# A decoder layer: loads issued by ScalarE instead of SyncE, two copies moved to VectorE, and new orders of work

## The chip, the cores and the metric

The kernel runs on one core of a Trainium2 chip. The metric is the device time of one execution in microseconds. The engines are called as in the profile: PE (TensorE), DVE (VectorE), ACT (ScalarE), POOL (GpSimd), SP (SyncE, which here only issues DMAs); "SPq" is the time of SP's queue in issuing them.

## The reference

One decoder layer in float32, for 32 batches of 112 rows of 256 numbers, with a context of 375 rows of 256 per batch:

```python
x = x + attn(layernorm(x), wq, wk, wv, wo)       # 8 heads of 128, q and k rms-normalised and rotated, causal
x = x + xattn(layernorm(x), ctx, ctx)            # gelu(xn @ ctx.T) @ ctx, per batch
x = x + ffn(layernorm(x), w1, b1, w2, b2)        # 256 -> 1024 -> 256, values rounded to 8 bits, relu
```

## The kernel before

Every engine has its own program: small functions, each one step for one batch `j` (a wait or several on semaphores, one or a few instructions, an increment of a semaphore), and three lists that call them, `start()`, `body(i)` for i from 5 to 25, and `end()`. The lists are written out by hand, and an engine goes through its list strictly in order. So a step that waits holds all that stand behind it on its engine. PSUM's eight banks are shared between steps, and part of the waits guard a bank until the step that read it is done.

The attention's input is laid out in tiles of 128 rows: eight batches of 112 rows make seven tiles, so 28 of the 32 batches have a tile of their own (`has_tile`), and in the other four the steps that work on tiles fall away. Precision is kept by splitting float32 values into two float16 parts (high, and the rest), which triples the matmuls of the projections, the scores and the output projection.

The steps of a batch, in the order in which its data passes, with the engine:

- SP `load_rows` brings the tile (`x_rows`); DVE `stats_x`, POOL `variance_x` and `root_x`, DVE `normalise_x` make `xn1`; ACT `round_xn` (L1455) makes its high half and DVE `split_xn` (L817) its low half; SP `transpose_x` is a DMA that transposes both into `xT16`.
- PE `project_q`, `project_k`, `project_v0`, `project_v1` (L1745). q and k go through ACT `square`, DVE `turn_cos`, `turn_sin`, `sum_squares`, the rotation's sum (DVE `turn_q`, POOL `turn_k`), POOL `rms_root`, ACT `scale` and `round`, DVE `split`, and then through DMA transposes issued by SP: `transpose_q`, `transpose_k`, and `transpose_q_next`, `transpose_k_next` for the rows of the tile that belong to the next batch.
- PE `scores`, ACT `softmax_exp`, POOL `mask_later_keys`, PE `weigh_values`, DVE `invert_sums`, ACT `normalise_o0`, `normalise_o1`, `round_o`, DVE `split_o` (L947), SP `transpose_o` (L321, a DMA), PE `project_out0` to `project_out3` (L1755), DVE `residual_attention`, which adds `x_in`, brought by SP `load_x` (L330).
- DVE `stats_x2`, POOL `root_x2`, DVE `normalise_x2`, PE `transpose_xn2`, ACT `copy_xn2T` (L1407, from PSUM to SBUF), PE `ctx_hidden` on the transposed context (`ctxT`, SP `load_ctxT`, L309), ACT `square_h`, DVE `gelu_inner`, ACT `tanh_h`, DVE `gelu_outer`, PE `ctx_out` on the context's rows (SP `load_ctx`, L335), DVE `residual_ctx`.
- DVE `stats_x3`, POOL `root_x3`, DVE `quantise_x3`, `clip_x3`, SP `transpose_xq` (a DMA), PE `hidden_units0`, `hidden_units1`, ACT `relu0`, `relu1`, DVE `clip_hidden`, PE `out_units`, POOL `add_b2`, DVE `residual_out`, SP `store_out`.

The steps of one round of `body` belong to several batches: on PE the projection of q runs three batches ahead of the round's number, `weigh_values` one ahead, `project_out` one behind, `out_units` four behind. All DMAs, of the weights too, are issued by SP, on one queue; those of one round are, in order: `load_ctxT`, `load_rows`, `transpose_o`, `transpose_x`, `load_x`, `load_ctx`, `transpose_q`, `transpose_k`, `transpose_q_next`, `transpose_xq`, `store_out`, `transpose_k_next`. Three of the loads wait until their buffer is free:

```python
def load_ctxT(j):
    if j.has(2):
        sp.wait_ge(h_ready, done(j.plus(-2)))
def load_x(j):
    if j.has(2):
        sp.wait_ge(x2_done, done(j.plus(-2)))
def load_ctx(j):
    if j.has(2):
        sp.wait_ge(ctxout_ready, done(j.plus(-2)))
```

Before the first batch, the weights are squared and summed (ACT `square_projection`, `square_wo`; PE `sum_weights`), scaled by a power of two, and rounded and split into halves (ACT `round_projection`, DVE `split_projection`).

Of the kernel before, what the change touches and what calls it, by code (L numbers as in the profile page):

```python
# [18 lines left out]
P = 128  # L19
BANK = 512  # L20
SLOTS = 4
# [42 lines left out]
def done(j):  # L64

    return j.off + 1
# [35 lines left out]
def decoder_layer(nc, x, ctx_rows, ctx_cols, wq, wk, wv, wo, w1_cols, b1, w2_cols, b2, tables, out):  # L102
# [30 lines left out]
    with ExitStack() as stack:  # L133
# [92 lines left out]
        y_ps = psum[0:T, 6, 0:M]  # L226
        xn2T_ps = psum[:, 2, 0:MC * T]
        h_ps = psum[0:SP, 2, 0:SC * T]
        ctx_ps = psum[0:T, 7, 0:M]
        f0_ps, f1_ps = psum[:, 0, 0:FC // 2 * T], psum[:, 1, 0:FC // 2 * T]  # L230
        f2_ps = psum[0:T, 7, 0:M]
# [40 lines left out]
        def _(sp):  # L272
# [33 lines left out]
            def load_ctxT(j):  # L306
                if j.has(2):
                    sp.wait_ge(h_ready, done(j.plus(-2)))
                sp.dma_start(ctxT[:, j.off % 2], ctx_cols[j.at].rearrange("o (c p) s -> (o p) c s", p=P)).then_inc(  # L309
                    ctxT_landed[j.off % SLOTS], 16)  # L310

            def load_rows(j):
                if 3 <= j.off <= 4:
                    sp.wait_ge(xn_done, done_t(j.plus(-2)))
                sp.dma_start(x_rows[:, tile_no(j) % 2, :], x_flat[tile_no(j)]).then_inc(rows_landed[tile_no(j) % 2], 16)

            def transpose_o(j):
                if j.has(1):
                    sp.wait_ge(y1_added, done(j.plus(-1)))
                sp.wait_ge(o_lo_done, done(j))  # L320
                sp.dma_start_transpose(oT16[:, :, :], o16[:, :, :].rearrange("t l n -> t (l n)")).then_inc(oT_landed, 16)  # L321

            def transpose_x(j):
                sp.wait_ge(xn_lo_done, done_t(j))
                sp.dma_start_transpose(xT16[:, :, tile_cols(j)], xn16[:, :, :].rearrange("t l n -> t (l n)")).then_inc(xT_landed, 16)

            def load_x(j):
                if j.has(2):
                    sp.wait_ge(x2_done, done(j.plus(-2)))
                sp.dma_start(x_in[:, j.off % SLOTS, :], x[j.at].rearrange("o t m -> (o t) m")).then_inc(x_landed[j.off % SLOTS], 16)  # L330

            def load_ctx(j):
                if j.has(2):
                    sp.wait_ge(ctxout_ready, done(j.plus(-2)))
                sp.dma_start(ctx_in[:, j.off % 2], ctx_rows[j.at].rearrange("o (p c) m -> (o p) c m", c=SC)).then_inc(  # L335
                    ctx_landed[j.off % SLOTS], 16)

            def transpose_q(j):
                sp.wait_ge(q_lo_done, done_t(j))
                own, cut = own_rows(j)  # L340
                sp.dma_start_transpose(qkT[:, j.off % 2, 0, :, PAD + own:PAD + T], qk16[0:cut, 0].rearrange("t l n -> t (l n)")).then_inc(qT_landed, 16)  # L341

# [5 lines left out]
            def transpose_q_next(j):  # L348
                sp.wait_ge(q_lo_done, done_t(j))
                if j.has(1):  # L350
                    sp.wait_ge(s_ready, done(j.plus(-1)))
                own, cut = own_rows(j)
                for a, b in pieces_after(cut):
                    sp.dma_start_transpose(qkT[:, (j.off + 1) % 2, 0, :, PAD + a - cut:PAD + b - cut],  # L354
                                           qk16[a:b, 0].rearrange("t l n -> t (l n)")).then_inc(qT_next_landed, 16)
# [1816 lines left out]
```

## Time and profile before

| what | value |
|---|---|
| median of 3 runs | 658.45 us (656.49 to 659.91) |
| the profiled execution's own time | 658.12 us |
| its span, from the first to the last instruction | 656.1 us |
| mean granted clock of TensorE | 0.972 |
| busy: PE, DVE, ACT, POOL | 583.0, 533.7, 526.5, 382.2 us |

Busy is the time in which an engine has an instruction in execution; the issuing of DMAs doesn't count. A batch with a tile takes about 18 us in the middle of the run, and the span is longer than 32 times the mean round by the filling and the draining of the pipeline.

### The profile page before, as it was taken

Reading aid. Unit: us, or ns where it says so; the run is one execution under the profiler, and the core shown is the slowest. Engines: PE = TensorE matmul, PEld = TensorE weight load, DVE = VectorE, ACT = ScalarE, POOL = GpSimd, SP = SyncE. Lnnn points to the kernel's source line nnn. Section 1 sums busy time; section 2 is a strip of 40 time slices with the busy share of each in tenths; the row PEclk is TensorE's granted clock in tenths of the full one; section 3 lists DMA queues with packets and bytes.
Section 4 is the critical chain, followed back from the end, with each engine's and each line's share of the span. In section 5 each row is a group of like instructions: output and inputs, shape, how many; then the busy total and the mean of one; then the engine's idle time right before and its main releaser. Section 6 shows DMA issues by size and latency. Waiting matters only on the chain.

```text
span 656.1 us, 13024 instructions
## 1 busy us (share of the span) xinstructions
PE 583.0 (89%) x4528; PEld 440.0 (67%) x4528; DVE 533.7 (81%) x1059; ACT 526.5 (80%) x1350; POOL 382.2 (58%) x402
## 2 busy tenths in 40 slices
PE   1678699898999999989999999989998888799984
PEld 1324367676777777776787777757777556589873
DVE  3898689797899998986999999967997879584653
ACT  6888689695899998994999999976898778696643
POOL 1445466582677776763678877733776649352321
PEclk9887799999999999999999999989999989899998
DMA  8665764898799999989889899998798969979551
GB/s 297 203 135 120 102 111 87 143 124 167 144 141 169 159 155 154 148 158 174 125 166 152 146 157 156 158 147 178 102 162 130 168 97 130 107 165 167 152 123 29
DMA packets 236720, 95.25 MB, mean 145 GB/s; under 512 B 210144, under 2 KB 231248, under 8 KB 236656
## 3 DMA queue, kind: packets, MB, share of 16 engines
q1 hardware_dynamic: 236656, 94.43, 82.3%
q8 instruction: 36, 0.59, 0.4%
q14 instruction: 28, 0.23, 0.1%
HBM read 39.08 MB, written 3.67 MB: 65 GB/s over the span
## 4 chain that ended last, share of the span: by engine, by line
PE 41%; SPq 22%; DVE 13%; DMA 8%; POOL 6%; ACT 6%; issue 3%; ACTq 0%; DVEq 0%
PE psum L1750 6%; PE psum L1751 5%; PE psum L1752 5%; PE psum L1911 4%; SPq L354 4%; PE psum L1880 3%; PE psum L1796 3%; SPq L321 3%; DMA qkT<-qk 3%; SPq L373 3%; SPq L346 3%; SPq L341 2%; PE psum L1758 2%; PE psum L1760 2%; PE psum L1759 2%
## 5 line engine op out<-in xcount | busy, mean ns | idle before, releaser
L1750 PE MATMUL psum<-wqkv,xT 128*128 128x512 f16 (+1 forms) x352 | 139.3, 396 | 16.7 <-DVE wqkv L772 9.3
L1751 PE MATMUL psum<-wqkv,xT 128*128 128x512 f16 (+1 forms) x352 | 138.8, 394 | 0.0
L1752 PE MATMUL psum<-wqkv,xT 128*128 128x512 f16 (+1 forms) x352 | 138.5, 393 | 0.0
L578 POOL TENSOR_TENSOR turn_c<-turn_c,turn_s 128x1024 f32<-128x1024 f32 x28 | 80.1, 2859 | 25.2 <-DVE turn_c L746 19.4
L753 DVE TENSOR_TENSOR turn_s<-psum,sin_t 128x1024 f32<-128x1024 f32 x56 | 68.0, 1216 | 11.9 <-ACT sq L1330 11.7
L1758 PE MATMUL psum<-wo,oT 128*112 128x256 f16 x256 | 70.0, 273 | 5.2 <-DMA oT<-o 5.2
L1750 PEld LDWEIGHTS psum<-wqkv,xT 128*128 128x128 f16 (+1 forms) x352 | 39.8, 113 | 51.0 <-DVE wqkv L772 9.5
L1760 PE MATMUL psum<-wo,oT 128*112 128x256 f16 x256 | 69.8, 273 | 0.0
L1759 PE MATMUL psum<-wo,oT 128*112 128x256 f16 x256 | 69.8, 273 | 0.0
L603 POOL TENSOR_TENSOR rms<-ms,nhalf 128x8 f32<-128x8 f32 x28 | 68.2, 2436 | 2.2
L595 POOL TENSOR_TENSOR rstd<-ve,nhalf 112x1 f32<-112x1 f32 x32 | 26.4, 826 | 72.7 <-DVE ve L864 72.7
L746 DVE TENSOR_TENSOR turn_c<-psum,cos_t 128x1024 f32<-128x1024 f32 x56 | 68.1, 1216 | 0.5 <-ACT sq L1427 0.4
L1752 PEld LDWEIGHTS psum<-wqkv,xT 128*128 128x128 f16 (+1 forms) x352 | 39.8, 113 | 40.9 <-issue 5.9
L1911 PE MATMUL psum<-v_sb,wo_raw 112*112 112x129 f32 x512 | 63.3, 275 | 2.6 <-issue 2.0
L1302 ACT ACTIVATE qk<-w_raw 128x1024 f16<-128x1024 f32 x56 | 59.6, 1064 | 3.5 <-DMA qkT<-qk 3.1
L1911 PEld LDWEIGHTS psum<-v_sb,wo_raw 112*112 112x112 f32 x512 | 58.8, 176 | 4.9 <-issue 3.5
L1751 PEld LDWEIGHTS psum<-wqkv,xT 128*128 128x128 f16 (+1 forms) x352 | 39.9, 113 | 32.9 <-issue 4.7
L1849 PE MATMUL psum<-qkT 128*112 128x112 f16 x256 | 42.9, 219 | 15.0 <-DMA qkT<-qk 13.6
L1434 ACT ACTIVATE w_raw<-turn_c,rms 128x128 f32<-128x128 f32 x112 | 35.8, 392 | 21.3 <-POOL rms L603 17.8
L1880 PE MATMUL psum<-ctx_all,g 125*112 125x256 f32 x192 | 48.7, 390 | 2.2 <-DVE g L955 1.6
L573 POOL TENSOR_TENSOR rms<-ms,nhalf 128x8 f32<-128x8 f32 x28 | 48.4, 1727 | 2.2
L1368 ACT ACTIVATE f_int<-psum,b_col 128x112 int16<-128x112 f32 x128 | 34.7, 360 | 16.9 <-PE psum L1868 16.9
(108 smaller groups left out, 1634.6 us busy)
## 6 DMA issues: line engine op xcount, KB each, us to landing
ctxT<-in_ctx_cols SPq DMA_DIRECT2D x32, 375.0 KB, 4.1
ctx_all<-in_ctx_rows SPq DMA_DIRECT2D x32, 375.0 KB
x_rows<-in_x SPq DMA_DIRECT2D x28, 128.0 KB, 3.8
x_in<-in_x SPq DMA_DIRECT2D x32, 112.0 KB, 2.7
out_y<-y_out SPq DMA_DIRECT2D x32, 112.0 KB, 2.1
w_raw<-in_w SPq DMA_DIRECT2D x2, 1024.0 KB, 6.2
qkT<-qk SPq DMA_TRANSPOSE x128, 4.3
w_raw<-in_wk SPq DMA_DIRECT2D x2, 512.0 KB, 4.8
```

The lines of the kernel that those rows point to most:

```text
L578: pool.tensor_tensor(turn_c[:, 1, :], turn_c[:, 1, :], turn_s[:, 1, :], ALU.add).then_inc(k_turned, 1)
L603: pool.tensor_tensor(rms[:, 0, :], ms[:, 0, :], nhalf[:, 0:H], ALU.pow).then_inc(q_rms_done, 1)
L746: return dve.tensor_tensor(turn_c[:, w, :].rearrange("t (h f) -> t h f", f=HALF), ps.rearrange("t b (h f) -> t (b h) f", f=HALF), table, A ...
L753: return dve.tensor_tensor(turn_s[:, w, :].rearrange("t (h two f) -> t h two f", two=2, f=HALF), halves, table, ALU.mult)
L1750: pe.matmul(dst, hi, wqkv[:, 0, c, w, cols], start=c == 0, stop=False)
L1751: pe.matmul(dst, hi, wqkv[:, 1, c, w, cols], start=False, stop=False)
L1752: last = pe.matmul(dst, lo, wqkv[:, 0, c, w, cols], start=False, stop=c == MC - 1)
L1758: pe.matmul(y_ps, oT16[:, h, :], wo16[:, 0, h, :], start=first and h == heads[0], stop=False)
L1759: pe.matmul(y_ps, oT16[:, h, :], wo16[:, 1, h, :], start=False, stop=False)
L1760: product = pe.matmul(y_ps, oT16[:, H + h, :], wo16[:, 0, h, :], start=False, stop=last and h == heads[-1])
L1880: last = pe.matmul(ctx_ps, g[:, c * T:(c + 1) * T], ctx_in[:, j.off % 2, c, :], start=c == 0, stop=c == SC - 1)
L1911: last = pe.matmul(o_ps[:, h // OH, at:at + VW], p_sb[:, h * T:(h + 1) * T], v_sb[:, h, :], start=h % OH == 0, stop=h % OH == OH - 1 or h ...
```

## The change

- `load_rows`, `load_ctxT`, `load_x` and `load_ctx` are issued by ACT, on its own DMA queue. The waits of `load_ctxT` and `load_x` are gone (the order of ACT's other steps stands in for them). SP keeps the weights, the transposes and the stores.
- `round_xn` and `copy_xn2T` run on DVE as `tensor_copy`.
- All lists are laid out anew, and PSUM's banks with them: `scores` and `v0`, `out_units` share banks, `weigh_values` and q, `ctx_hidden` and `ctx_out`, and `w_sum_ps` now lies in a bank of `k_ps`. So the first `project_k` waits for the last of the weights' sums, `w_sq_done[3]`, that of wo. The waits that guard banks follow.
- In the loop, on PE, q runs one batch ahead of the round's number, `weigh_values` one behind, `project_out` two behind, `transpose_xn2` three, `ctx_out` four, `out_units` five. `project_out` begins with `project_out2`.

```diff
-        q_ps, k_ps = psum[:, 4:6, :], psum[:, 0:2, :]
-        v0_ps, v1_ps = psum[0:T, 7, :], psum[0:T, 3, :]
-        s_ps = psum[0:T, 0:2, 0:HH * T]
-        o_ps = psum[0:T, 4:7, 0:OH * VW]
+        q_ps, k_ps = psum[:, 1:3, :], psum[:, 5:7, :]
+        v0_ps, v1_ps = psum[0:T, 4, :], psum[0:T, 3, :]
+        s_ps = psum[0:T, 4:6, 0:HH * T]
+        o_ps = psum[0:T, 0:3, 0:OH * VW]
...
+            def load_rows(j):
+                if j.has(2):
+                    act.wait_ge(xn_done, done_t(j.plus(-2)))
+                act.dma_start(x_rows[:, tile_no(j) % 2, :], x_flat[tile_no(j)]).then_inc(rows_landed[tile_no(j) % 2], 16)
...
+            def load_ctxT(j):
+                act.dma_start(ctxT[:, j.off % 2], ctx_cols[j.at].rearrange("o (c p) s -> (o p) c s", p=P)).then_inc(
+                    ctxT_landed[j.off % SLOTS], 16)
...
+            def load_x(j):
+                act.dma_start(x_in[:, j.off % SLOTS, :], x[j.at].rearrange("o t m -> (o t) m")).then_inc(x_landed[j.off % SLOTS], 16)
...
+            def load_ctx(j):
+                if j.has(2):
+                    act.wait_ge(ctxout_ready, done(j.plus(-2)))
+                act.dma_start(ctx_in[:, j.off % 2], ctx_rows[j.at].rearrange("o (p c) m -> (o p) c m", c=SC)).then_inc(
+                    ctx_landed[j.off % SLOTS], 16)
...
+            def round_xn(j):
+                dve.wait_ge(xn_done, done_t(j))
+                if j.has(1):
+                    dve.wait_ge(xT_landed, 16 * done_t(j.plus(-1)))
+                dve.tensor_copy(xn16[:, 0, :], xn1[:, :]).then_inc(xn_hi_done, 1)
...
+            def copy_xn2T(j):
+                dve.wait_ge(xn2T_ready, done(j))
+                dve.tensor_copy(xn2T[:, :, :].rearrange("p c t -> p (c t)"), xn2T_ps).then_inc(xn2T_copied, 1)
```

The loops after the change, in order, without the conditions on tiles (c is the batch i+1, d i, e i-1, f i-2, g i-3, h i-4, and i itself i-5; a and b are i+3 and i+2):

```
SP    transpose_q d, transpose_q_next d, transpose_k d, transpose_o e, transpose_k_next d, transpose_x a,
      store_out i, transpose_xq g
PE    project_q c, ctx_out h, transpose_xn2 g, hidden_units1 i, hidden_units0 i, scores e, ctx_hidden g,
      project_out2 f, project_out0 f, project_out1 f, project_out3 f, out_units i, weigh_values e,
      project_k c, project_v0 d, project_v1 d
ACT   square_h h, scale_k1 e, scale_k0 e, tanh_h h, round_k0 e, normalise_o0 f, normalise_o1 f, round_o f,
      square_k d, copy_v0 e, load_rows a, scale_q0 d, load_ctxT f, copy_v1 e, scale_q1 d, load_x e, square_q c,
      relu1 i, relu0 i, load_ctx f, round_q0 d, softmax_exp e
DVE   normalise_x b, turn_q d, split_k e, gelu_outer h, split_o f, turn_cos_k d, normalise_x2 g, turn_sin_k d,
      round_xn b, sum_squares_k d, residual_ctx h, copy_xn2T g, stats_x3 h, stats_x a, turn_sin_q c,
      clip_hidden1 i, quantise_x3 h, clip_x3 h, clip_hidden0 i, split_xn b, turn_cos_q c, sum_squares_q c,
      gelu_inner g, residual_attention f, residual_out i, split_q d, invert_sums e, stats_x2 f
POOL  root_x3 i, rms_root_k e, mask_later_keys f, variance_x b, root_x b, add_b2 i, rms_root_q d, root_x2 g,
      turn_k d
```

In `start()`, SP issues wv, wk, wq, wk, wq in halves, then wo, the biases and the other half of wv, and ACT at the same time the first context, two tiles of rows and the first x.

## Rows read from the trace of the kernel before

**Rows 1.** The page: part 1, PE's line, and part 4, the chain by engine.

```profile
PE 583.0 (89%) x4528; PEld 440.0 (67%) x4528; DVE 533.7 (81%) x1059; ACT 526.5 (80%) x1350; POOL 382.2 (58%) x402
...
PE 41%; SPq 22%; DVE 13%; DMA 8%; POOL 6%; ACT 6%; issue 3%; ACTq 0%; DVEq 0%
```

**Rows 2.** Windows of one batch, 18 of them, 181.30 to 505.63: busy us, clock, DMA.

```profile
342.31:360.25 17.94, 17.94 (x148) 13.81 (x145) 17.16 (x35) 16.73 (x46) 14.04 (x13) 1.00 0.95 158
...
sum 324.33, PE 316.51 PEld 243.99 DVE 290.43 ACT 284.21 POOL 224.33; mean PE 17.58 PEld 13.55 DVE 16.13 ACT 15.79 POOL 12.46
```

**Rows 3.** Windows of 30 us: length, then busy us by engine as in rows 2.

```profile
0.00:30.00 30.00, 10.73 (x40) 6.09 (x40) 16.10 (x36) 21.35 (x29) 7.73 (x21) 0.99 0.80 268
...
540.00:570.00 30.00, 23.97 (x191) 17.79 (x192) 21.39 (x35) 22.62 (x56) 18.82 (x16) 0.94 0.85 122
```

**Rows 4.** Waits of PE: who waited for whom, us in total, times, longest.

```profile
PE psum L1849 <- DMA qkT<-qk: 13.6, 9, 4.3
...
PE psum L1868 <- DMA xqT<-xq: 6.1, 2, 3.3
...
PE psum L1758 <- DMA oT<-o: 5.2, 3, 2.4
```

**Rows 5.** Timeline of SP in the undisturbed batch: start, us of issuing, line.

```profile
343.41 0.57 SPq L330 DMA_DIRECT2D x_in<-in_x  x1
344.03 0.33 SPq L335 DMA_DIRECT2D ctx_all<-in_ctx_rows  x1
...
347.55 3.39 SPq L346 DMA_TRANSPOSE qkT<-qk  x1
...
355.48 1.34 SPq L309 DMA_DIRECT2D ctxT<-in_ctx_cols  x1
356.87 0.47 SPq L315 DMA_DIRECT2D x_rows<-in_x  x1
357.43 2.73 SPq L321 DMA_TRANSPOSE oT<-o  x1
```

**Rows 6.** Groups by line and shape: busy us, mean ns, idle before.

```profile
L817 DVE TENSOR_TENSOR xn<-xn 128x256 f16<-128x256 f32 x28 | 16.1, 575 | 1.6 <-ACT xn L1302 1.6
...
L920 DVE SCALAR_TENSOR_TENSOR y_out<-psum,x3b 112x256 f32<-112x256 f32 x32 | 13.2, 412 | 8.6 <-PE psum L1788 8.6
...
L1302 ACT ACTIVATE xn2T<-psum 128x224 f32<-128x224 f32 x32 | 12.0, 374 | 4.1 <-PE psum L1765 3.9
...
L1302 ACT ACTIVATE xn<-xn 128x256 f16<-128x256 f32 x28 | 11.4, 408 | 0.5 <-DVE xn L932 0.3
...
L804 DVE TENSOR_SCALAR b_rows<-b_clip 112x256 f32<-112x256 f32 x1 | 0.3, 286 | 0.0
```

**Rows 7.** Timeline of PE in a batch: start, us, line (weigh_values, out_units, project_out).

```profile
181.31 1.98 PE L1911 MATMUL psum<-v_sb,wo_raw 112*112 112x129 f32 x16
...
185.91 1.04 PE L1788 MATMUL psum<-w2T,f_q 128*112 128x256 bf16 x8
...
188.08 0.27 PE L1758 MATMUL psum<-wo,oT 128*112 128x256 f16 x1
188.19 0.27 PE L1759 MATMUL psum<-wo,oT 128*112 128x256 f16 x1
```

**Rows 8.** Timelines of ACT and DVE in the undisturbed batch: normalise_o1, round_o, split_o.

```profile
345.99 1.16 ACT L1421 ACTIVATE wo_raw<-psum,rden 112x128 f32<-112x128 f32 x4
...
351.19 1.04 ACT L1302 ACTIVATE o<-wo_raw 112x1024 f16<-112x1024 f32 x1
...
352.58 1.22 DVE L947 TENSOR_TENSOR o<-wo_raw,o 112x1024 f16<-112x1024 f32 x1
```

**Rows 9.** The tile oT: its transposes, from issue to landing.

```profile
DMA to landing us min/median/max: 4.0/5.4/8.5
```

**Rows 10.** DMA issues: the load of wo, us from issue to landing last.

```profile
wo_raw<-in_wo SPq DMA_DIRECT2D x1, 1024.0 KB, 10.3
```

**Rows 11.** Timeline of PE at the start: the first project_k.

```profile
16.96 0.61 PE L1750 MATMUL psum<-wqkv,xT 128*128 128x512 f16 x1 [3.69 <-DVE wqkv L772]
```

More of the change, by code:

```diff
@@ L1423, in normalise_o1, with round_o @@
                 last.then_inc(o1_normed, 1)
+            def round_o(j):
+                act.wait_ge(o1_normed, done(j))
+                if j.has(1):
+                    act.wait_ge(oT_landed, landed_once(j.plus(-1)))
+                act.wait_ge(o0_normed, done(j))
+                copy(o16[:, 0, :], on[:, :]).then_inc(o_hi_done, 1)
             def square_k(j):
@@ L1830, in project_out3, with ctx_out, transpose_xn2 @@
-            def project_out3(j):
-                project_out(range(6, 8), j, first=False, last=False).then_inc(y_ready, 1)
+            def ctx_out(j):
+                pe.wait_ge(ctx_landed[j.off % SLOTS], landed(j))
+                pe.wait_ge(g_done, done(j))
+                for c in range(SC):
+                    last = pe.matmul(ctx_ps, g[:, c * T:(c + 1) * T], ctx_in[:, j.off % 2, c, :], start=c == 0, stop=c == SC - 1)
+                last.then_inc(ctxout_ready, 1)
+            def transpose_xn2(j):
+                pe.wait_ge(xn2_done, done(j))
+                if 1 <= j.off <= B - 10 or j.off == B - 4:
+                    pe.wait_ge(v1_copied, done(j.plus(2)))
+                if j.off == B - 7 or j.off == B - 5:
+                    pe.wait_ge(x2_done, done(j.plus(1)))
+                if j.off == 0:
+                    pe.wait_ge(ident_in, 16)
+                transpose_rows(xn2T_ps, xn2).then_inc(xn2T_ready, 1)
@@ new lines, in hidden_units1 @@
+            def hidden_units1(j):
+                pe.wait_ge(xqT_landed, landed_once(j))
+                if B - 6 <= j.off <= B - 5:
+                    pe.wait_ge(o1_normed, done(j.plus(3)))
+                if j.off == B - 4:
+                    pe.wait_ge(o0_normed, done(j.plus(3)))
+                for c in range(1 * FC // 2, 2 * FC // 2):
+                    for m in range(MC):
+                        last = pe.matmul(f1_ps[:, (c % (FC // 2)) * T:(c % (FC // 2) + 1) * T], w1T[:, m, c, :], xqT[:, m, :],
+                                         start=m == 0, stop=m == MC - 1)
+                last.then_inc(f1_ready, 1)
@@ L1852, in scores, with ctx_hidden @@
                 last.then_inc(s_ready, 1)
-            def project_out2(j):
-                project_out(range(4, 6), j, first=False, last=False).then_inc(y2_added, 1)
-            def project_out1(j):
-                project_out(range(2, 4), j, first=False, last=True).then_inc(y1_added, 1)
-            def hidden_units1(j):
-                pe.wait_ge(xqT_landed, landed_once(j))
-                if j.off <= B - 10:
+            def ctx_hidden(j):
+                pe.wait_ge(ctxT_landed[j.off % SLOTS], landed(j))
+                pe.wait_ge(xn2T_copied, done(j))
+                if j.off == B - 6 or j.off == B - 4:
+                    pe.wait_ge(x3_done, done(j.plus(-1)))
+                for c in range(SC):
+                    for m in range(MC):
+                        last = pe.matmul(h_ps[:, c * T:(c + 1) * T], ctxT[:, j.off % 2, m, c * SP:(c + 1) * SP], xn2T[:, m, :],
+                                         start=m == 0, stop=m == MC - 1)
+                last.then_inc(h_ready, 1)
```

1841 lines of the change are left out of this document (894 added, 947 removed).

## The prediction

> **What bounds the kernel now.** I read the page's first and fourth part first [rows 1]: TensorE is busy for 583 us of a span of 656.1, and no other engine comes near enough to be the bound on average. The chain that ended last spends 41% on PE, but 22% on SPq (SyncE issuing DMAs) and 8% on landings of DMAs. So the kernel has two faces, and windows separate them. Over the 18 batches between 181.30 and 505.63 us TensorE is busy 316.51 of 324.33 us: 7.8 us idle in half of the run [rows 2]. One undisturbed batch there takes 17.94 us, all of it TensorE at full clock, with VectorE at 17.16, ScalarE at 16.73, GpSimd at 14.04 and the DMA engines at a share of 0.95 [rows 2]. This stretch is bound by TensorE, which the change leaves as it is: the matmuls are the same. The rest of the idle 73.1 us (656.1 less 583.0) lies at the two ends: 19.3 us in the first 30 alone and 6.0 in the 30 from 540 [rows 3].
>
> The waits say what TensorE stands for: of its idle time 13.6 us end with the landing of a transposed q or k, 6.1 with that of xq and 5.2 with that of o, 24.9 us together [rows 4]. These transposes are issued by SP, one after the other, between the loads. SP's queue in the undisturbed batch shows loads of 0.57 (x_in), 0.33 (ctx rows), 1.34 (ctxT) and 0.47 us (x_rows), 2.71 together, beside transposes of which one takes 3.39 and another 2.73 us [rows 5]. A load in front of a transpose delays it by its issue, and by its wait where the buffer isn't free yet.
>
> **The change, part by part.** The profiled execution took 658.12 us, 2.0 more than its span, and 0.3 less than the median of the runs (658.45). The sum starts from 658.1. A difference of 0.5% (3.3 us) is about what a measurement of this kernel tells from none.
>
> *Four loads per batch leave SP.* SP gets 2.71 us per batch back, and no transpose stands behind a load's wait on x2_done, h_ready or ctxout_ready. In the undisturbed batches this is worth nothing, since TensorE is never waiting there. What it can reach is the 24.9 us of waits for transposes. Ends: nothing, if the landing is late because the DMA engines are full (a share of 0.95), and 20 us, if the issue decides (a fifth of the 24.9 kept back, since behind an earlier landing the next wait is seldom far). I take 14, nearer the upper end, since the chain counts 22% for issuing and 8% for landing. The Trainium skill, "DMA: Bandwidth & Descriptors", section "Issuing engines are not separate DMA queues", says that DMAs of all issuing engines run on the same 16 DMA engines and interleave, so that a second issuer saves issue time only. By that rule alone the gain would be the lower end; the share of 0.95 agrees with it, the 22% speaks for a real part of issue time.
>
> *ScalarE issues them.* Before, no ScalarE DMA is in the trace. Its work falls by the rounding of xn (0.408) and the copy of xn2T (0.374 us) [rows 6], 0.78 together, to 15.95 in a batch of 17.94: 2.0 us are free. Four issues at SP's prices are 2.71, at the shortest that SP shows (0.33) 1.3. If an issue runs ahead of the arithmetic queued on ScalarE, it costs nothing. So ScalarE comes to 15.95 + 2.71 = 18.7 us in the dear case, without a gap: 0 to +0.7 us for each of 28 batches with a tile, 0 to +20 us. I take 0: x and ctxT are now loaded with no wait in front of them, x_rows and ctx rows wait for things a batch old, and their places are behind copies and ReLUs of some 0.5 to 1 us that keep the engine fed. The cover is the 2.0 us; beyond 0.5 us per issue it is gone.
>
> *VectorE takes the rounding and the copy.* Neither is in the trace. Round_xn lies between 0.286 (a 112x256 f32 copy with a factor, L804) and 0.575 (the 128x256 subtraction to f16, L817); the copy from PSUM between 0.286 and 0.412 (the 112x256 residual from PSUM, L920) [rows 6]. That is 0.57 to 0.99. I take 0.7: the plain copy is nearer to L804, that from PSUM to L920. VectorE comes to 17.16 + 0.7 = 17.9 of 17.94: still under TensorE, but full. Ends: 17.7, which costs nothing, and 18.15, +0.2 us for 28 batches, 6 us.
>
> *The orders.* In the loop a batch now goes from weigh_values to project_out in one round, where it took two. Between the end of weigh_values and the first project_out lies one round less the matmuls of project_out (24 at 0.11 from start to start, 2.6 us), out_units (1.0) and weigh_values (2.0) [rows 7]: 17.94 - 5.6 = 12.3 us. In them o must be normalised (two groups of 1.16), rounded (1.04), split (1.22) [rows 8] and transposed, 5.4 us from issue to landing in the median and 8.5 at most [rows 9]: 10.0 us, 13.1 with the longest. It fits by 2.3 us as long as ScalarE, VectorE and SP come to it at once; behind project_out all else waits, so what it is late is late for the round. Similarly copy_xn2T stands on VectorE between residual_ctx, which waits for ctx_out, and ctx_hidden, which waits for the copy. I charge 2 us for such slips (0 to +10), as most batches keep both margins.
>
> *The start.* The first project_k now shares a PSUM bank with the sums of the weights and waits for w_sq_done[3], so for the load of wo (10.3 us from issue to landing) [rows 10] and its squares, where it started at 16.96 us and waited for w_k alone [rows 11]. With wo issued sixth it can't start before about 20. But TensorE stood idle again in the same 30 us, 19.3 in all, so part is taken from that idle time: 0 to +5, I take +2.
>
> Sum: 658.1 - 14 + 0 + 0 + 2 + 2 = 648.1.
>
> **The rivals.** *The transfers are the limit, not SP.* For it: a DMA share of 0.95 in a batch in which nothing waits, and a k transpose whose issue took 3.39 us. Against it: loads of 0.33 and 0.47 us pass through the same queue in the same batch, so it isn't full throughout, and the chain gives SPq nearly three times the landings' share. The 14 us shrink to some 3, and 2 + 2 take them back: 659, from 656 to 661.
>
> *ScalarE becomes the bound*, on the other side. Its issues last as long as SP's or longer, drawn out as SP's 3.39 us is. The place is between copy_v0 and softmax_exp, the price each microsecond past 2.0 per batch; late exp delays the mask, out_units and weigh_values at once. At 0.9 us per issue (between SP's 0.33 and 1.34) it is 3.6, less 2.0 a plus of 1.6 for 28 batches, 45 us, with the 10 us gained elsewhere 693; it decides from 2.4 us of issues per batch, where the 10 us are eaten. For it: ScalarE's 16.73. Against it: 0.33 to 0.57 for three of four of SP's loads. The Trainium skill, "Perfetto Trace Analysis", section "DMA Instruction — HWDGE (DVE, Sync)", has a sequencer wait for a lock on a descriptor generator that two of them share, and the profile's duration includes that wait; no row here shows two issuers, so it can't be seen whether ScalarE would stand behind a 3.39 us transpose.
>
> *The loop of o or VectorE sets the round.* If o's transpose lands a microsecond later than the median at each batch, or VectorE waits 0.5 us more than its fullness allows, the round is 0.5 us longer: 28 x 0.5 = 14, so 648 + 14 = 662, and up to 672 where both meet. For it: landings up to 8.5. Against it: SP has 2.71 us less to do.
>
> *The ends shorten too.* SP's relief gives all 20 us and the fill and drain, shorter by the round that o saves, some 10 more: 658 - 20 - 10 = 628, up to 636. Against it: the first matmul is later, and the drain is one chain through all engines.
>
> **How the numbers follow.** SP relieved, covers hold: 0.44, 648, from 638 to 655. Transfers the limit: 0.14, within 0.5%. ScalarE the bound: 0.21, 665 to 720. The loop of o or VectorE: 0.13, counted as slower. The ends too: 0.08. Faster 0.44 + 0.08 = 0.52, same 0.14, slower 0.21 + 0.13 = 0.34. The range from 632 to 680 leaves out half of the last case (0.04) and what of ScalarE's lies above 680 (0.13); the likeliest case's own is 638 to 655.
>
> **What would show it.** Right: SPq's share of the chain falls well under 22%; PE's waits for qkT, xqT and oT fall from 24.9 to near 11 us; a batch in the middle still takes 17.9 to 18.0 with PE busy throughout, VectorE near 17.9; ScalarE's DMA issues last under 0.5 us and nothing on it waits behind them; the first project_k starts past 20 us. Wrong: rounds of 18.3 us or more; ScalarE's queue in the chain with issues near or over 1 us; PE idle before project_out for oT in each round; or the same waits for qkT at the same length with SP idle before them, which would make it the transfers.

## The result and the profile after

The changed kernel takes 726.77 us (median of 4 runs, 725.50 to 729.12) where the kernel before took 657.47 beside it: a ratio of 1.105, 95% interval 1.101 to 1.110. The forecast was 648, from 632 to 680, with "faster" at 0.52. It was wrong in sign and by 79 us. (The profiled executions of a_early_exp, a_early_late_exp and a_early_wsum, below, were disturbed by the chip, so of these three only the ratio, which leaves such executions out, is used for the time.)

The page of the changed kernel, part 1 and the chain by engine of part 4, as in [rows 1]:

```profile
PE 604.2 (83%) x4528; PEld 462.7 (64%) x4528; DVE 544.9 (75%) x1119; ACT 514.7 (71%) x1290; POOL 355.2 (49%) x402
...
PE 31%; DMA 29%; DVE 18%; SPq 12%; ACT 4%; POOL 3%; issue 3%; ACTq 0%; DVEq 0%; POOLq 0%
```

SP's issuing fell from 22% of the chain to 12%, as the change intends. What grew in its place is the landing of DMAs, 8% to 29%. By its share of the span no engine is fuller than before: ScalarE fell to 514.7 us (71%) and VectorE is at 75%.

The waits of PE in the changed kernel, as in [rows 4] (L1839 is scores, L1757 project_out, L1805 hidden_units1):

```profile
PE psum L1839 <- DMA qkT<-qk: 35.0, 12, 10.7
PE psum L1757 <- DMA oT<-o: 20.9, 16, 4.2
...
PE psum L1805 <- DMA xqT<-xq: 4.7, 1, 4.7
```

The three tiles that the prediction wanted to see fall from 24.9 to 11 us rose to 60.6.

Windows from one weigh_values to the next in the changed kernel, 20 of them, from batch 5 (159.06) to batch 25 (557.00), columns as in [rows 2]:

```profile
177.72:195.63 17.91, 17.91 (x146) 13.83 (x145) 14.87 (x33) 14.74 (x40) 10.66 (x13) 1.00 0.45 98
...
455.40:480.51 25.11, 19.86 (x134) 16.34 (x133) 14.47 (x33) 16.02 (x42) 11.68 (x13) 0.80 0.96 114
...
sum 397.94, PE 363.50 PEld 281.75 DVE 322.07 ACT 301.22 POOL 218.69; mean PE 18.18 PEld 14.09 DVE 16.10 ACT 15.06 POOL 10.93
```

And the same 20 batches of the kernel before, in one window:

```profile
145.56:505.63 360.07, 350.54 (x2824) 270.31 (x2821) 318.38 (x644) 310.62 (x820) 240.87 (x241) 1.00 0.93 153
```

Five of the 20 rounds still take 17.9 us, with PE busy throughout. The others take from 16.3 to 25.1 (the shortest is the last, whose steps are mostly those of the list `end()`). Of the 37.9 us that these batches lost, 24.9 are idle time of PE (34.4 now, 9.5 before). The other 13.0 are busy time (363.50 against 350.54) for nearly the same matmuls (2789 against 2824): the granted clock fell from 1.00 to 0.96, and in the round of 25.11 us to 0.80.

Split at the same two batches, the 67.6 us by which the span grew (656.1 to 723.7) are 13.5 before batch 5 (159.06 against 145.56), 37.9 in the 20 rounds, and 16.2 behind batch 25 (166.7 against 150.5). In what follows these are the start, the loop and the drain.

**Where the loop's time goes.** The chain that ended last, in the round of 25.11 us of the changed kernel (start, us, what):

```profile
455.60 0.42 DVE y_out L872
456.02 1.14 DVE qk L877
457.16 0.02 issue
457.18 1.20 SPq L309
...
458.48 1.22 SPq L317
...
459.75 1.32 SPq L317
...
461.11 2.00 SPq L323
...
463.21 12.26 DMA oT<-o
475.47 0.04 issue
475.51 0.46 PE psum L1757
...
479.80 0.87 PE psum L1880 x8
```

It is a circle. L1880 is out_units. When it ends, VectorE can do residual_out (y_out, L872), and behind that split_q (L877) in its list. Only then may SP transpose q (L309), q_next (two pieces, L317) and k (L323), and behind them o, which takes 12.26 us from issue to landing. Then project_out runs, and behind it out_units again, 25.1 us after the last one. project_out's first matmuls start 0.21 us apart, not 0.11: the granted clock fell from 1.00 while PE stood idle for 3.50 us ahead of the scores (L1839), is 0.50 from 469.0 to 478.6 us, the lower of its two levels (1.2 GHz), and then 1.00 again:

```profile
468.99 0.34 PE L1839 MATMUL psum<-qkT 128*112 128x112 f16 x1 [3.50 <-DMA qkT<-qk]
```

```profile
469.00:478.60 9.60, 8.18 (x51) 7.92 (x52) 1.07 (x4) 4.07 (x11) 2.91 (x5) 0.50 1.37 133
```

The timelines of ACT, DVE and SP in that round show that split_q's own input was ready long before (the bracket is the idle time of the engine just before, and what ended it):

```profile
466.89 1.11 ACT L1266 ACTIVATE qk<-w_raw 128x1024 f16<-128x1024 f32 x1
```

```profile
474.62 0.50 DVE L858 SCALAR_TENSOR_TENSOR h_t<-h_sq,psum 125x336 f32<-125x336 f32 x1 [5.05 <-ACT h_sq L1294]
...
479.84 0.48 DVE L863 SCALAR_TENSOR_TENSOR x<-psum,y_unit,x_in 112x256 f32<-112x256 f32 x1 [4.72 <-PE psum L1759]
480.71 0.42 DVE L872 SCALAR_TENSOR_TENSOR y_out<-psum,x3b 112x256 f32<-112x256 f32 x1 [0.39 <-PE psum L1880]
481.06 1.22 DVE L877 TENSOR_TENSOR qk<-w_raw,qk 128x1024 f16<-128x1024 f32 x1
```

```profile
476.09 1.90 SPq L351 DMA_TRANSPOSE xqT<-xq  x1
482.30 1.13 SPq L309 DMA_TRANSPOSE qkT<-qk  x1
```

round_q0 ended at 468.00, and split_q began at 481.06: for 13 us it stood behind gelu_inner (L858), residual_attention (L863) and residual_out, for which VectorE waited 5.05, 4.72 and 0.39 us. The last two waited for PE itself, gelu_inner for ScalarE's square_h, which needs ctx_hidden, and that stands behind the scores on PE. SP had nothing else to issue from 477.99 to 482.30. Then q, q_next, k, o and k_next come at once, and o is behind the first three. ScalarE's loads of x_rows, ctxT and x fall into the same time, issued at 461.26, 461.84 and 462.72 where o's transpose is issued at 463.21; how much of the 12.26 us is theirs this round doesn't show.

### The profile page after: what moved, and what is told of

Same layout as the page of the kernel before. It is cut to its first block, busy times and chain, and to the rows that moved or that the text cites. A ratio compares the mean times of both kernels' runs of the same rounds, so it can differ in the third digit from the quotient of the medians.

```text
span 723.7 us, 12992 instructions
## 1 busy us (share of the span) xinstructions
PE 604.2 (83%) x4528; PEld 462.7 (64%) x4528; DVE 544.9 (75%) x1119; ACT 514.7 (71%) x1290; POOL 355.2 (49%) x402
## 4 chain that ended last, share of the span: by engine, by line
PE 31%; DMA 29%; DVE 18%; SPq 12%; ACT 4%; POOL 3%; issue 3%; ACTq 0%; DVEq 0%; POOLq 0%
DMA oT<-o 18%; DMA qkT<-qk 5%; SPq L317 4%; PE psum L1896 4%; PE psum L1757 3%; PE psum L1749 3%; SPq L323 3%; PE psum L1751 3%; PE psum L1750 3%; PE psum L1758 3%; PE psum L1759 3%; DMA xT<-xn 3%; PE psum L1880 3%; SPq L309 2%; DVE turn_s L685 2%
## 5 line engine op out<-in xcount | busy, mean ns | idle before, releaser
L1749 PE MATMUL psum<-wqkv,xT 128*128 128x512 f16 (+1 forms) x352 | 137.8, 392 | 19.9 <-DMA xT<-xn 6.6
L1750 PE MATMUL psum<-wqkv,xT 128*128 128x512 f16 (+1 forms) x352 | 137.2, 390 | 0.0
L1751 PE MATMUL psum<-wqkv,xT 128*128 128x512 f16 (+1 forms) x352 | 136.9, 389 | 0.0
L540 POOL TENSOR_TENSOR turn_c<-turn_c,turn_s 128x1024 f32<-128x1024 f32 x28 | 66.2, 2364 | 99.4 <-DVE turn_s L685 76.3
L1757 PE MATMUL psum<-wo,oT 128*112 128x256 f16 x256 | 74.5, 291 | 21.0 <-DMA oT<-o 20.9
L521 POOL TENSOR_TENSOR x3b<-x,b_rows 112x256 f32<-112x256 f32 x32 | 40.0, 1251 | 91.0 <-DVE y_out L872 91.0
L1839 PE MATMUL psum<-qkT 128*112 128x112 f16 x256 | 48.5, 235 | 38.5 <-DMA qkT<-qk 35.0
L1758 PE MATMUL psum<-wo,oT 128*112 128x256 f16 x256 | 73.6, 287 | 0.0
L1759 PE MATMUL psum<-wo,oT 128*112 128x256 f16 x256 | 73.4, 287 | 0.0
L1330 ACT ACTIVATE wo_raw<-psum,rden 112x128 f32<-112x128 f32 x128 | 36.5, 371 | 47.6 <-DVE rden L885 47.5
L1266 ACT ACTIVATE qk<-w_raw 128x1024 f16<-128x1024 f32 x56 | 60.0, 1072 | 11.1 <-DMA qkT<-qk 10.6
L1839 PEld LDWEIGHTS psum<-qkT 128*112 128x112 f16 x256 | 37.7, 147 | 42.0 <-DMA qkT<-qk 37.3
L863 DVE SCALAR_TENSOR_TENSOR x<-psum,y_unit,x_in 112x256 f32<-112x256 f32 x32 | 15.4, 481 | 57.3 <-PE psum L1759 44.0
L529 POOL TENSOR_TENSOR rms<-ms,nhalf 128x8 f32<-128x8 f32 x28 | 56.4, 2016 | 2.2
L1433 ACT ACTIVATE wo_raw<-psum 112x896 f32<-112x896 f32 x32 | 29.9, 934 | 37.8 <-PE psum L1841 34.0
```

Source lines behind the costliest of these rows:

```text
L540: pool.tensor_tensor(turn_c[:, 1, :], turn_c[:, 1, :], turn_s[:, 1, :], ALU.add).then_inc(k_turned, 1)
L1266: return act.activation(dst, src, ACT.Copy)
L1749: pe.matmul(dst, hi, wqkv[:, 0, c, w, cols], start=c == 0, stop=False)
L1750: pe.matmul(dst, hi, wqkv[:, 1, c, w, cols], start=False, stop=False)
L1751: last = pe.matmul(dst, lo, wqkv[:, 0, c, w, cols], start=False, stop=c == MC - 1)
L1757: pe.matmul(y_ps, oT16[:, h, :], wo16[:, 0, h, :], start=first and h == heads[0], stop=False)
```

## The experiments

Three theories at first: the new orders, the second queue (ScalarE's loads delay SP's transposes), and engines that are too full (ScalarE by its issues, VectorE by its two copies). All kernels were timed beside the kernel before on the same chip; "ratio" is to that. Of each kernel's profile I give start, loop and drain, split as above (before: 145.6, 360.1, 150.5; changed: 159.1, 397.9, 166.7).

**One part alone.** b_loads_act, edits of the kernel before:

```diff
 # SP body: load_ctxT(f), load_rows(a), load_x(e), load_ctx(g) taken out;  ScalarE body:
                 copy_v0(e)
+                load_ctxT(f)
+                if a.has_tile():
+                    load_rows(a)
...
                 relu1(i)
+                load_x(e)
+                load_ctx(g)
```

> The kernel before, with the four loads of the loop's 21 rounds issued by ScalarE at the same moment as SP did (ctxT and x_rows behind copy_v0, x_in and ctx rows behind relu1), all else as before. Theory of the orders (the new lists bunch the transposes and leave o and q, k too little time; the queue and the copies are innocent): 648 to 660 us, within 0.5% or a little faster, transposes landing as before (oT 5.4 us median). Theory of the second queue (loads of ScalarE compete with SP's transposes for the same DMA engines): 680 to 700, oT's median towards 7.0 us. Theory of ScalarE's issues: 670 or more, with ScalarE waiting behind its own DMAs.

Measured: ratio 1.004 (0.998 to 1.009); loop 364.6. So the loads alone bring nothing. But the landings of oT and xT did lengthen (us from issue to landing, min/median/max; before they were 4.0/5.4/8.5 [rows 9] and 2.4/3.1/5.3):

```profile
DMA to landing us min/median/max: 4.0/7.8/14.5
DMA to landing us min/median/max: 2.4/6.5/12.0
```

The old order has room for a transpose that lands 2 to 3 us later. The queue theory was right on the landings and wrong on the time.

b_copies_dve, the other part alone:

```diff
 # ScalarE body: copy_xn2T(g) and round_xn(a) taken out;  VectorE body:
                 invert_sums(e)
+                copy_xn2T(g)
...
+                if a.has_tile():
+                    round_xn(a)
                 gelu_inner(g)
```

> The kernel before, with round_xn and copy_xn2T of the loop's 21 rounds on VectorE, loads on SP as before. Theory of the orders: 655 to 664, VectorE near 17.9 us of a batch of 17.94 and no round over 18.2. Theory that VectorE is too full: 0.5 us or more per round, 670 or more.

Measured: ratio 1.0025 (0.9989 to 1.0060); loop 366.6. No difference in the time that can be told. The expectation of no round over 18.2 us failed: in this trace nine of the 20 rounds are longer, up to 20.05 us, where three are in the kernel before.

**One part undone.** a_loads_sp puts the loop's loads back on SP in the changed kernel, each for one batch further ahead than ScalarE issued it, a_copies_act the two copies back on ScalarE:

```diff
 # a_loads_sp: the four loads taken out of ScalarE's body;  SP body (e.g. n = i+4):
                     transpose_k_next(d)
+                load_rows(n)
+                load_ctxT(e)
                 transpose_x(a)
+                load_x(d)
                 store_out(i)
+                load_ctx(e)
 # a_copies_act: out of VectorE's body;  ScalarE body:
                 copy_v0(e)
+                round_xn(b)
...
                 copy_v1(e)
+                copy_xn2T(g)
```

> The changed kernel, with the loop's four loads back on SP (ctxT and x_rows behind transpose_k_next, x behind transpose_x, ctx rows behind store_out), the new orders kept. Theory of the orders: no better than 727, 720 to 745, since SP now has 2.7 us per round more before o and k_next. Theory of the second queue: 670 to 690, transposes landing as in the kernel before.

> The changed kernel, with round_xn and copy_xn2T of the loop back on ScalarE (behind copy_v0 and copy_v1), the new orders and the queue kept. ctx_hidden waits for x3_done of the batch before in every batch, since the copy no longer orders the shared bank. Theory of the orders: 720 to 735, no change that matters. Theory that VectorE is too full: 690 or less.

Measured: 1.112 (1.106 to 1.118) and 1.103 (1.093 to 1.114), against 1.105 of the changed kernel. Nothing comes back. Of the three theories the orders are left, though a_loads_sp has a fault of its own, as will be seen.

**Cutting the circle.** Two cuts at different places, and one edit that shortens the way without cutting it. a_o_older leaves out the wait for the o just transposed and uses the one before, with the same work:

```diff
 # a_split_q_early, VectorE body
                     sum_squares_q(c)
+                if d.has_tile():
+                    split_q(d)
                 gelu_inner(g)
                 residual_attention(f)
                 residual_out(i)
-                if d.has_tile():
-                    split_q(d)
 # a_o_older, project_out2 (oT16 with two buffers, project_out reads the older)
-                pe.wait_ge(oT_landed, landed_once(j))
+                pe.wait_ge(oT_landed, landed_once(j.plus(-1) if j.has(1) else j))
 # a_qnext_late, SP body (a_early_late: this and a_split_q_early)
                     transpose_q(d)
-                    transpose_q_next(d)
                     transpose_k(d)
                 transpose_o(e)
+                    transpose_q_next(d)
                     transpose_k_next(d)
```

> The changed kernel with one step moved in VectorE's loop: split_q d stands ahead of gelu_inner, residual_attention and residual_out, where it stood behind them; nothing else. Theory of the closed circle (split_q waits behind residual_out for out_units, out_units stands behind project_out, project_out waits for oT, whose transpose queues behind those of q, q_next and k, which wait for split_q): the circle is cut, SP issues q and q_next in its idle time before, and the 21 rounds of the loop lose most of their 2.2 us each: 675 to 695 us. Theory of o's short way alone (weigh_values to project_out in 12.3 us): 715 to 730, since nothing on o's own way is changed.

> The changed kernel, but project_out of a batch reads the transposed o of the batch before (two buffers of oT; the first batch reads its own), so it never waits for a transpose just issued; the output is that of a shifted o, the work is the same. Theory of o's short way: every wait for oT is gone and the rounds come back to 17.9 to 18.2, 675 to 685. Theory of the circle: it still closes over the scores, which wait for the q and k that split_q holds and stand ahead of project_out, so only part comes back: 695 to 715, and PE's waits for qkT stay at 30 us or more.

> The changed kernel with one step moved in SP's loop: transpose_q_next d is issued behind transpose_o, not ahead of k and o. Theory of the circle: the way from split_q to o is shorter by what q_next takes on SP and on the DMA engines (about 2.6 us of issue), but the circle is not cut: 700 to 720. Theory that the load queue delays o: no change, 722 to 732.

> Both moves together: split_q early on VectorE and q_next behind o on SP. Theory of the circle: as split_q early alone, or up to 5 us less, 672 to 695. Theory of o's short way: as q_next late alone.

| kernel | median us | ratio (95%) | loop |
|---|---|---|---|
| a_split_q_early | 695.0 | 1.060 (1.053 to 1.067) | 366.9 |
| a_o_older | 698.3 | 1.062 (1.057 to 1.068) | 367.6 |
| a_qnext_late | 757.4 | 1.152 (1.145 to 1.160) | 424.9 |
| a_early_late | 758.3 | 1.154 (1.147 to 1.160) | 430.8 |

Either cut gives back 30 to 31 of the loop's 37.9 us: PE's idle time falls from 34.4 to 16.6 us (a_split_q_early) and 16.9 (a_o_older), and its busy time comes back to 350.3 and 350.7. The loop of a_split_q_early:

```profile
156.37:523.30 366.93, 350.29 (x2788) 270.50 (x2787) 322.03 (x673) 300.66 (x777) 208.22 (x241) 0.99 0.88 147
```

It isn't one circle, though, but two that share split_q and out_units: one over o, the other over the scores, which wait for q and k and stand ahead of project_out. In the loop of the changed kernel PE waits 17.7 us for q and k and 15.3 for o, in a_split_q_early 1.2 and 10.8, in a_o_older 13.4 and nothing. The expectation for a_o_older had this second way, and came true in the time (698) and in PE's wait for q and k over the whole span, "30 us or more":

```profile
PE psum L1839 <- DMA qkT<-qk: 32.6, 11, 12.4
```

That two cuts which end different waits give nearly the same is not explained, and both together were not tried. o's short way alone is refuted by a_split_q_early, which changes nothing on o's own way (695 us, where that theory said 715 to 730), and by a_o_older (698, where it said 675 to 685).

a_qnext_late, expected at 700 to 720 us, came at 757, and a_early_late, expected at 672 to 695, at 758. The waits of ACT in the first say why (L1266 is the line of round_q0 and round_k0):

```profile
ACT qk L1266 <- DMA qkT<-qk: 69.5, 17, 9.3
```

In the changed kernel that wait is 10.6 us. round_q0 of the next batch may not overwrite q before q_next has landed, and ScalarE's softmax_exp and all that follows stand behind it. So q_next is not idle cargo: it is on a third circle. I put softmax_exp ahead of round_q0 to test that:

```diff
 # a_early_exp (with split_q early), a_early_late_exp (with both moves), ScalarE body
                 load_ctx(f)
+                softmax_exp(e)
                 if d.has_tile():
                     round_q0(d)
-                softmax_exp(e)
```

> The changed kernel with split_q early, and on ScalarE's loop softmax_exp e ahead of round_q0 d, where it stood behind it. Theory of the long circle (round_q0 waits for the landed q and q_next of the batch before and holds softmax_exp, for which out_units waits): the 20 rounds from batch 5 to 25, 366.9 us, come closer to the 358.8 of undisturbed ones, 686 to 694 us in all. Rival, that exp ahead delays round_q0 and so q: 697 or more.

> The kernel with split_q early and q_next late (758 us), and softmax_exp e ahead of round_q0 d. Theory of the long circle, that q_next late cost 62 us because round_q0 of the next batch waits for its landing and holds softmax_exp and out_units behind it: most of it comes back, 690 to 715 us. If q_next's landing holds the scores or SP's queue itself: 745 to 760.

Measured: 1.054 (1.046 to 1.062) and 1.099 (1.086 to 1.111). The first gains nothing that can be told. The second returns from 1.154, about half of the loss and less than expected: the wait of round_q0 is still 66 us, and other steps stand behind it on ScalarE; which of them pays wasn't tested. So softmax_exp behind round_q0 is a part of the third circle, not all of it.

**The loads in the new orders.** Is the relief of SP worth something there, or in the drain of the old order?

```diff
 # b_loads_act_all: b_loads_act, and the drain's loads moved in the same way
 # a_early_loads_sp: a_split_q_early with the edit of a_loads_sp
 # a_early_rows_first: the same, SP body:
+                load_rows(n)
                 transpose_q(d)
...
                 transpose_k_next(d)
-                load_rows(n)
                 load_ctxT(e)
```

> The kernel before, old orders, with the four loads issued by ScalarE in the loop and in the drain, at about the moments at which SP issued them, waits kept. The prediction's term (SP's relief ends part of the 24.9 us of PE's waits for transposes, most of them at the ends): 640 to 652 us. Theory that transposes and loads share DMA engines and SP's issue time is not what PE waits for: 655 to 668, as with the loop's loads alone.

> The changed kernel with split_q early (695 us) and the loop's loads back on SP. With the circle closed this move cost 9 us (736 to 727). Theory that SP's relief counts where transposes are bunched in the new orders: again 5 to 15 us slower, 700 to 710. Theory that it counted only through the circle: 692 to 699.

> The changed kernel with split_q early and the loop's loads on SP (733 us), load_rows moved from behind k_next to the head of SP's round. Theory of the place (VectorE's stats_x stood 77 us waiting for x_rows, and clip_hidden and out_units behind it): most of the 38 us comes back, 692 to 706, and VectorE's wait for x_rows falls under 20 us. Theory that SP's issue time itself is short in the new orders: 715 or more.

Measured: 1.011 (1.004 to 1.019), drain 150.8; 1.111 (1.103 to 1.120), loop 408.3; 1.030 (1.024 to 1.037), median 679.3, loop 357.3. a_early_loads_sp missed both of its ranges. The wait of VectorE's stats_x for x_rows, first in a_early_loads_sp and a_loads_sp, then in a_early_rows_first:

```profile
DVE stat L842 <- DMA x_rows<-in_x: 77.4, 16, 10.3
```

```profile
DVE stat L842 <- DMA x_rows<-in_x: 76.4, 16, 7.8
```

```profile
DVE stat L842 <- DMA x_rows<-in_x: 8.3, 1, 8.3
```

So it was the place that I had given load_rows, not SP's load of work, that made a_early_loads_sp slow. a_loads_sp has the same wait: its 720 to 745 came true by luck, and it told nothing of the queue. With load_rows in a good place the kernel with the loads on SP is faster than that with the loads on ScalarE: 1.030 against 1.060. oT lands in 4.9 us in the median against 6.2, xT in 2.9 against 4.1. That the second queue as such is the reason is not shown, since the loads also stand at other moments. In a_split_q_early ScalarE issues x_rows, ctxT and x at 196.56, 197.13 and 198.01, around o's transpose at 197.94; in a_early_rows_first x_rows, o's transpose and ctxT are issued at 191.51, 198.64 and 202.88. ScalarE's loads at such moments were not tried. The loop's window is then 2.8 us shorter than that of the kernel before, but holds 35 matmuls less, and PE is busy 3.2 us less in it; its idle time, 10.0 us, is about that of before (9.5):

```profile
154.77:512.07 357.30, 347.31 (x2789) 267.37 (x2788) 319.30 (x673) 300.59 (x778) 206.01 (x242) 1.00 0.84 152
```

**The drain.** In a_split_q_early PE waits 12.7 us for the k and q of the batch B-2. ScalarE's queue just before, and windows of 5 us (columns as in [rows 2]):

```profile
606.44 0.40 ACTq L1373 DMA_DIRECT2D ctxT<-in_ctx_cols  x1
...
606.89 0.41 ACTq L1417 DMA_DIRECT2D ctx_all<-in_ctx_rows  x1
...
607.77 0.27 ACTq L1417 DMA_DIRECT2D ctx_all<-in_ctx_rows  x1
608.07 1.06 ACTq L1373 DMA_DIRECT2D ctxT<-in_ctx_cols  x1
609.16 0.65 ACTq L1391 DMA_DIRECT2D x_in<-in_x  x1
```

```profile
610.00:615.00 5.00, 2.63 (x29) 2.37 (x27) 0.75 (x5) 4.62 (x14) 0.00 (x0) 1.00 1.23 129
615.00:620.00 5.00, 0.00 (x0) 0.00 (x0) 0.00 (x0) 0.00 (x0) 0.00 (x0) 0.58 1.25 135
620.00:625.00 5.00, 0.00 (x0) 0.00 (x0) 0.21 (x1) 0.00 (x0) 0.00 (x0) 0.50 1.31 128
```

Four context loads of 375 KB and one of 112 KB, 1.6 MB, are issued within 3.4 us, while SP issues q_next, k and k_next. From 615 to 624 no engine computes. Taking the burst apart:

```diff
 # a_early_spread (with split_q early), a_spread_only (without), ScalarE end
                 load_ctxT(Batch(B - 5))
+                load_x(Batch(B - 4))
                 load_ctx(Batch(B - 5))
-                load_ctx(Batch(B - 4))
-                load_ctxT(Batch(B - 4))
-                load_x(Batch(B - 4))
...
                 softmax_exp(Batch(B - 2))
+                load_ctx(Batch(B - 4))
+                load_ctxT(Batch(B - 4))
 # a_spread2: load_ctx(Batch(B - 5)) behind softmax_exp(Batch(B - 2)) too
```

> The changed kernel with split_q early (695 us), and in the drain ScalarE's burst of five loads taken apart: x of the batch B-4 first, ctx rows of B-5, and ctx rows and ctxT of B-4 only behind softmax_exp of B-2. Theory of the burst (1.4 MB of loads issued within 3 us meet the q_next, k and k_next transposes of B-2 on the same DMA engines, which then run at a share of 1.25 for 15 us while every engine stands still): PE's wait of 12.7 us for qkT in the drain falls to 4 to 8 us, 686 to 691 us. Theory that the 128 rows of q_next and k_next fill the DMA engines by themselves: wait and time as before, 693 to 698.

> As split_q early with the drain's burst taken apart (685 us), the load of ctx rows of B-5 taken out of it too, behind softmax_exp of B-2: two loads are left of five (12.7 us of wait for qkT in the drain with five, 6.4 with three). Theory of the burst: the wait falls to 3 to 5 us, 682 to 685. If the transposes alone take the rest: 6 us as before, 685.

> The changed kernel, with only the drain's burst of five loads taken apart (three, and two behind softmax_exp of B-2), split_q where it was. Theory of the burst: the part behind batch 25 (166.7 us) shortens by 3 to 7, the total to 719 to 724. If the burst is not what the drain waits for: 725 to 729.

| kernel | wait for qkT of B-2 | drain | ratio (95%) |
|---|---|---|---|
| the changed kernel | 10.7 | 166.7 | 1.105 (1.101 to 1.110) |
| a_split_q_early | 12.7 | 167.0 | 1.060 (1.053 to 1.067) |
| a_early_spread | 6.4 | 162.4 | 1.037 (1.030 to 1.045) |
| a_spread2 | under 2 | 164.0 | 1.057 (1.051 to 1.064) |
| a_spread_only | 7.8 | 161.1 | 1.100 (1.095 to 1.105) |

The wait follows the size of the burst, and the drain is 3 to 6 us shorter in each trace. But in the kernels that keep the drain's list it lies anywhere from 162.2 us (a_early_loads_sp) to 171.1 (a_o_older), so this is not clear of the scatter. In the totals the effect is unclear: only the first shows it (5.2 us of its trace's 9.8 are gained ahead of the drain, where the edit changes nothing, and a_spread_xq below, which has the same edit, is at 1.054), the third dose moves a wait to the last batch, and a_spread_only (median 725.9) can't be told from the changed kernel.

**The start.**

```diff
 # a_early_wsum (with split_q early): the bank of the sums; sum_weights(3) behind project_q(0)
-        w_sum_ps = psum[:, 6, 0:4]
+        w_sum_ps = psum[:, 7, 0:4]
 # a_spread_xq (a_early_spread), SP start
+                transpose_xq(Batch(0))
                 transpose_q_next(Batch(4))
                 transpose_q(Batch(4))
                 transpose_k(Batch(4))
-                transpose_xq(Batch(0))
```

> The changed kernel with split_q early, and the sums of the weights in bank 7 of PSUM instead of a bank of k; the first project_k and project_q stand ahead of the sum of wo's squares, and VectorE bounds wo's sum behind split_projection. Theory that the bank delays the start: the first project_k starts 2 to 5 us sooner than the 22.4 us of the changed kernel, and the total falls by 2 to 5, 690 to 693. Theory that other things set the start (the order of the weights' loads, VectorE's splits): the first project_k comes sooner, the first weigh_values not, 694 to 697.

> As split_q early with the burst taken apart (685 us), and in SP's start list transpose_xq of batch 0 ahead of q_next, q and k of batch 4, behind which it stood and landed some 14 us after xq was ready. Theory that SP's order in the start makes the first hidden units wait: batch 3 to 4 (24.5 us) shortens by 4 to 6 us and the total to 679 to 682. Theory that the start is set by the weights and by VectorE: no change.

Measured: 1.056 (1.044 to 1.067) and 1.054 (1.045 to 1.062), no gain in either. The first project_k of the changed kernel, as in [rows 11], started at 22.41 us:

```profile
22.41 0.61 PE L1749 MATMUL psum<-wqkv,xT 128*128 128x512 f16 x1 [0.25 <-DVE w_sq L690]
```

With the other bank it starts at 20.94, 1.5 us sooner and not 2 to 5. With xq first, PE's wait of 3.9 us for xqT in a_early_spread is gone, and waits of 1.8 us for qkT and 2.3 for oT stand in its place: batch 3 to 4 takes 24.1 us after 24.5. One transpose moved ahead of others makes those late.

## Why the prediction was wrong, point by point

**Four loads leave SP, -14.** Wrong in sign: with the loop's loads moved the old order is no faster (1.004), with the drain's too 1.1% slower (0.4 to 1.9), and the drain is as long as it was (150.8 against 150.5): PE's waits there for qkT and xqT, 5.4 and 3.3 us of the 24.9, are now 7.0 and 3.3. In the new orders, with the circle cut, the kernel with the loads on SP is the faster one (1.030 against 1.060). The step that failed is the choice "nearer the upper end, since the chain counts 22% for issuing and 8% for landing". The share of the chain says on what the chain lay, not what a microsecond less of it gives. So the first sign of being right, SPq's share well under 22%, came true (12%) in a kernel that is 10% slower. The DMA engines' share of 0.95 [rows 2] was the better witness. The Trainium skill, "DMA: Bandwidth & Descriptors", section "Issuing engines are not separate DMA queues", says that DMAs of all issuers interleave on the same 16 engines; oT's 5.4 to 7.8 us in b_loads_act agrees. The prediction used that rule for a lower end of nothing; that a second queue can make the first one's transposes slower was not in the sum at all. The rival "the transfers are the limit" (0.14, 656 to 661) describes this part alone well; it was drowned by the orders.

**ScalarE issues them, 0.** Right. Issues last 0.27 to 1.3 us and run beside the arithmetic (below). ScalarE as the bound, the rival of 0.21, is refuted: it is busy 301 of the loop's 398 us.

**VectorE takes two copies, 0.** Right as far as the time can tell (b_copies_dve, 1.0025, though the loop of its trace is 6.6 us longer), and in size: 0.29 and 0.38 us, 0.68 together where 0.7 was taken ([rows 6] gave the bounds). Rows by line and shape of the changed kernel:

```profile
L796 DVE COPY xn2T<-psum 128x224 f32<-128x224 f32 x32 | 12.3, 384 | 8.8 <-PE psum L1764 8.8
...
L781 DVE CAST xn<-xn 128x256 f16<-128x256 f32 x28 | 8.2, 292 | 0.0
```

**The orders, +2 (0 to +10).** This term failed most: 37.9 us in the loop, most of it here, and part of the drain's 16.2. The budget of 12.3 us for o was worked out along o's own steps, with each server free "as long as ScalarE, VectorE and SP come to it at once". They don't: on SP o stands behind q, q_next and k, so all four wait for split_q, and split_q stands in VectorE's list behind gelu_inner, residual_attention and residual_out. In the round of 25.11 us o's transpose took 12.26 us from issue to landing, where 5.4 to 8.5 were taken; the sign named for it, PE idle before project_out for oT, is there in 13 of the 20 rounds, 15.3 us together. The lists in the front part show all of this. What was not done was to follow each wait of one round into the next, until it closes. The rival "the loop of o or VectorE sets the round" named the right family with 0.13; its price of 0.5 us per round measured 1.9.

**The start, +2 (0 to +5).** The first project_k came at 22.41, past 20 as said, and the first weigh_values 4.2 us later (61.26 against 57.05), inside the bounds. That the shared bank is the reason is not borne out by a_early_wsum, whose interval is too wide for 2 us. And the late first project_k is made up by the weigh_values of batch 2, at 91.62 us against 92.88. The 13.5 us by batch 5 are lost behind it. The windows to batch 2 and from there to batch 5, of the changed kernel and of the kernel before:

```profile
0.00:91.62 91.62, 56.07 (x300) 32.00 (x301) 69.29 (x109) 68.47 (x133) 44.11 (x54) 0.94 0.66 154
91.62:159.06 67.44, 56.32 (x424) 44.70 (x423) 50.04 (x104) 47.79 (x121) 33.57 (x38) 0.92 0.86 137
```

```profile
0.00:92.88 92.88, 58.40 (x300) 32.16 (x301) 68.15 (x101) 70.74 (x140) 44.27 (x54) 0.89 0.68 164
92.88:145.56 52.68, 48.45 (x383) 37.18 (x383) 47.16 (x87) 44.62 (x117) 32.29 (x34) 1.00 0.73 114
```

Of the 14.8 us that the second window is longer, 7.9 are PE's busy time, with 41 more matmuls in it and a lower clock, and 6.9 its idle time. In a_split_q_early 2.7 of the 13.5 are gone. What makes the rest, and the some 11 us of the drain that neither circle nor burst explains, stays open; the lists of both ends differ throughout, and I did not take them apart.

"The ends shorten too" is refuted: both grew. None of the kernels tried beats the kernel before. Of those with the new orders the nearest, a_early_rows_first, is 3.0% slower: PE's idle time in its loop is that of before, and its ends are 24.1 us longer (154.8 + 165.4 against 145.6 + 150.5).

## What to carry to other kernels

When orders are laid out anew, follow each step to what it stands behind on its own engine, and that to what it waits for, until the way comes back to the same step one round later. The length of each such circle is a lower bound of the round, and an average of busy shares doesn't show it. Price a second DMA issuer by what it does to the landings of the first, not only by the issue time saved.

## What the runs showed of the hardware

ScalarE's DMA issues don't interrupt its arithmetic. The timeline of ACT in the changed kernel (start, us; ACTq is the queue):

```profile
460.81 1.00 ACT L1350 ACTIVATE sq<-psum 128x1024 f32<-128x1024 f32 x1
461.26 0.37 ACTq L1362 DMA_DIRECT2D x_rows<-in_x  x1
461.71 0.59 ACT L1266 ACTIVATE v_sb<-psum 112x512 f32<-112x512 f32 x1
461.84 0.54 ACTq L1373 DMA_DIRECT2D ctxT<-in_ctx_cols  x1
462.19 0.69 ACT L1368 ACTIVATE w_raw<-turn_c,rms 128x128 f32<-128x128 f32 x2
```

The issue of x_rows lies within the square, that of ctxT overlaps the copy, and the arithmetic follows without a gap. load_rows stands behind copy_v0 in the list (here the copy at 461.71), yet its issue starts 0.45 us ahead of it: the issue ran ahead of the arithmetic, the case in which the prediction charged nothing.

A high DMA share doesn't stand for one rate: in the drain's burst it was 1.25 at 135 GB/s, in an undisturbed batch of before 0.95 at 158 [rows 2].

With PE's idle time its busy time grew as well. In the loop 24.9 us more of idle time came with 13.0 us more of busy time for nearly the same matmuls, at a granted clock of 0.96 against 1.00; with split_q early the idle time falls from 34.4 to 16.6 us, and the busy time is 350.29 us again, at 0.99.
